# Two cross-attentions with keys projected into the heads' 8 channels, and quotients taken out of PSUM in all four

## The chip, the cores and the metric

The kernel runs on one core of a Trainium2 chip. The metric is the time of one execution on the device, in microseconds (us); the time before is the median of three runs.

## The reference

A tensor `x` of 32 batches x 56 tokens x 128 channels passes four layers. Each layer adds a cross-attention of its normalised tokens to a context of 32 batches x 1500 tokens x 64 channels, and then a feed-forward part. All four cross-attentions have 16 heads; their head width is 64, 8, 8 and 32. The second (the third is the same with biases):

```python
def _L1_xattn_ref(x, z, Wq, Wkv, Wo):        # x: 32 x 56 x 128, z: 32 x 1500 x 64
    Q = (x @ Wq.T).reshape(B, xN, 16, 8)
    KV = (z @ Wkv.T).reshape(B, zN, 2, 16, 8)
    K, V = KV[:, :, 0], KV[:, :, 1]
    attn = jax.nn.softmax(jnp.einsum('bqhd,bkhd->bhqk', Q, K) * 8 ** -0.5, axis=-1)
    return jnp.einsum('bhqk,bkhd->bqhd', attn, V).reshape(B, xN, 128) @ Wo.T

x = x + _L0_xattn_ref(_layernorm(x), ctx_512, ...)   # heads of 64
x = x + _L0_ffn_ref(_layernorm(x), ...)              # experts
x = x + _L1_xattn_ref(_layernorm(x), ctx_512, ...)   # heads of 8
x = x + _L1_ffn_ref(_layernorm(x), ...)              # int8 product
x = x + _L2_xattn_ref(_layernorm(x), ctx_512, ...)   # heads of 8, biases
x = x + _L2_ffn_ref(_layernorm(x), ...)              # Fourier
x = x + _L3_xattn_ref(_layernorm(x), ctx_512, ...)   # heads of 32
x = x + _L3_ffn_ref(_layernorm(x), ...)              # routed blocks
```

## The kernel before

The five engines' programs are written out by hand, with semaphores between them. Every float32 operand of a large product is held as a bf16 pair, high and remainder.

**Folded weights.** Before each cross-attention `pe_fold` multiplies every head's query weights with its key weights (line 242) and its value weights with its output weights (line 255). So a query has 64 channels per head, those of the context, and keys and values are the context itself. For heads of 8 channels too, a score is a sum over 64 context channels, and both parts of each pair count.

**A cross-attention** (`pe_cross`, `act_cross`, `dve_cross`, `pool_cross`, one queue of transfers in `sp_cross`) goes through 32 batches, each with 12 steps of 125 keys: 384 steps `T`, and two batches share a cycle of 24 steps, a pair. Columns are 16 heads x 56 queries = 896. In step `T`:

- TensorE takes up to two products (`product`) of a batch that comes later, then two halves of 448 score columns (`hf`), each by two matmuls: 128 rows (`cs`, high and remainder of the context, with the high queries `Qh`) and 65 rows (`chx` with the query remainders `Ql` and a row for the shift). Then it adds the values of step `T - 2`: for each of seven blocks of 128 columns, the high exponentials times 129 value columns (64 high, ones, 64 remainder), and the exponentials' remainder times 65.
- ScalarE takes the exponentials of both halves (line 751) into `pf`, one of three buffers.
- VectorE (line 823) and GpSimd (line 545) make the remainder `pl` of the exponentials of step `T - 1`; `JP` says how many of the seven blocks VectorE takes (5, 4, 4, 4). Both wait for both halves.

The products bound the scores from above, for the shift inside the exponential: a batch's 21 products of 500 columns (`PLAN`: for each of seven blocks a difference `d`, a sum `s` and a rest `r`) go through two PSUM banks. ScalarE turns the `d` (line 699), VectorE reduces `s` and `r` (lines 775, 778). The result is transposed, rounded and sent as one row into the query tile (line 436).

**The quotients of a batch.** The seven blocks of sums lie side by side in PSUM (129 columns each, over two banks, one set). After the last step of the batch ScalarE copies them out in two parts (lines 730, 731), GpSimd adds the halves (line 552), multiplies by the reciprocal that VectorE took (lines 802, 558), copies to bf16 (565) and makes the remainder (570). The first values of the next batch wait for the copies (`fc`). For the last batch VectorE does the four operations itself (lines 807 to 815). Transposes and the output product follow in a pair's later steps (`slot`), through PSUM bank 7, as do the projections of the queries: eight groups of two heads, three matmuls of 56 columns each, a fourth for the bias in the third cross-attention.

**Queries** go from `qch` and `qcl` to their place by six transfers a batch (`sp_spread`, lines 389 to 393), all on SP's queue, with the loads of `cs`, `chx` and the values `cnb` (lines 486 to 496). SP waits in the order of its program.

**Around it.** `pe_f1`, `act_f1` and `dve_f1` (the int8 part) also make the bias row `qbrow` of the third cross-attention (lines 1469, 1492). At the start SP loads inputs and the first weights and then the output bias (line 886), which the first `pe_fold` waits for.

Of the kernel before, what the change touches and what calls it, by code (L numbers as in the profile page):

```python
# [20 lines left out]
JP = (5, 4, 4, 4)  # L21
# [4 lines left out]
RND = 12582912.0  # L26

# [14 lines left out]
def build(nc, a, out):  # L42
    with ExitStack() as ctx:
# [54 lines left out]
        raw = [wst[:, 4032 + 903 * i:4935 + 903 * i].rearrange("p (j c) -> p j c", j=NJ) for i in range(2)]  # L98
# [8 lines left out]

        ctxN, ctxT = a["ctxN"], a["ctxT"]
# [7 lines left out]
        oneb = sb("oneb", [128, 64], BF16)  # L116
        qch, qcl = ([v[:, 12 + i, 0:448] for i in range(2)] for v in (Qh, Ql))
        qbrow = big[:, 6272:6784].bitcast(BF16)
# [112 lines left out]
        jobs1 = (0, 2, 4, 6, 10)  # L231
# [5 lines left out]
        def pe_fold(t, w, f, n, nd, wq, wk, wv, wo, weights, value):  # L237
            per = 512 // n
            w.wait_ge(weights, value)
            for j in range(H // per):  # L240
                for i in range(per):
                    r = t.matmul(bank(4 + j)[:, n * i:n * i + n], wq[0:nd, per * j + i, :], wk[0:nd, per * j + i, :],  # L242
                                 start=True, stop=True, skip_group_check=True)
                r.then_inc(s["f1"], 1)
            for j in range(4):
                k = fold_bank(f, n, j)
                if f in EARLY and j >= 2:
                    w.wait_ge(s["f1a"], FOLD_A[f])
# [10 lines left out]
        CLEAR_A1, CLEAR_MLP, CLEAR_F4 = 4, 11, 15  # L259
        EARLY = (1, 2)  # L260
        FOLD_A = (2, 6, 10, 12, 14)
# [39 lines left out]
        def act_fold(e, w, f, n):  # L301
            per, copies = 512 // n, 128 // n
            for j in range(1 if f == 3 else 0, H // per, 2 if f == 3 else 1):
# [23 lines left out]

        def pool_weights_low(g, w, f):
# [6 lines left out]
        def pool_fold(g, w, f):  # L335
            pool_weights_low(g, w, f)
# [45 lines left out]

        def sp_spread(y, w, ci, k):
            u, o = k % 2, k % QB
            w.wait_ge(s["pa"], B * ci + k + 1)
# [5 lines left out]
            w.wait_ge(s["pd"], B * ci + k + 1)  # L391
# [3 lines left out]
        def wait_spread_high(w, ci, k):  # L395
            w.wait_ge(s[f"qd_{k % 2}"], 64 * (B // 2 * ci + k // 2 + 1))

        def wait_spread_low(w, ci, k):
            w.wait_ge(s[f"ql_{k % 2}"], 32 * (B // 2 * ci + k // 2 + 1))
# [105 lines left out]
        def wait_tops(w, ci, k):  # L505
            w.wait_ge(s[f"lx_{k % 2}"], 16 * (ci * B // 2 + k // 2 + 1))
# [7 lines left out]
        def zeroed(ci):  # L514
            return 6 + 3 * ci if ci >= 0 else 0

        def pool_cross(g, w, ci):
            for k in range(2):
                g.memset(chx[k][64:65, :], 1.0).then_inc(s["zo"], 1)
                w.wait_ge(s["zo"], zeroed(ci - 1) + k + 1)  # L520
            for k in range(0 if ci else 3):
# [4 lines left out]
            for T in range(-36, NT + 11):  # L526
# [15 lines left out]
                if 0 <= T - 1 < NT:  # L542
                    r, at = (T - 1) % 3, 128 * JP[ci]
# [4 lines left out]
                if 0 <= (k := due(T, KT + 4)) < B - 1:  # L548
                    u, kb = k % 2, B * ci + k
                    r = raw[u][:, :, 0:C]  # L550
                    w.wait_ge(s["fc"], 2 * (kb + 1))
                    g.tensor_tensor(r, r, raw[u][:, :, C + 1:], ALU.add).then_inc(s["fp"], 1)  # L552
                    w.wait_ge(s["fp"], 4 * kb + 1)
                if 0 <= (k := due(T, KT + 7)) < B - 1:
                    u, kb = k % 2, B * ci + k
                    r = raw[u][:, :, 0:C]
                    w.wait_ge(s["rd"], kb + 1)
                    g.tensor_tensor(r, r, per_row(rden[u][:, :], C), ALU.mult).then_inc(s["fp"], 1)  # L558
                    w.wait_ge(s["fp"], 4 * kb + 2)
                if 0 <= (k := due(T, KT + 8)) < B - 1:  # L560
                    u, kb = k % 2, B * ci + k
                    r = raw[u][:, :, 0:C]
                    if k >= HB:
                        w.wait_ge(s["otr"], kb - HB + 1)
                    g.tensor_copy(O[:, k % HB, :, 0:C], r).then_inc(s["fp"], 1)
                    w.wait_ge(s["fp"], 4 * kb + 3)
                if 0 <= (k := due(T, KT + 10)) < B - 1:
                    u, kb = k % 2, B * ci + k
                    r = raw[u][:, :, 0:C]
                    g.tensor_tensor(O[:, k % HB, :, C:], r, O[:, k % HB, :, 0:C], ALU.subtract).then_inc(s["fp"], 1)  # L570
                    w.wait_ge(s["fp"], 4 * kb + 4)

        def pe_cross(t, w, ci, xh_, xl_, biased=False):
            t0, b0 = NT * ci, B * ci
            evac = (2 * NT + B) * ci

            def project(k):
                at = 128 * (k // 2) + 64 * (k % 2)
                hi, lo = xh_[:, at:at + NQ], xl_[:, at:at + NQ]
                for g in range(H // 2):  # L580
                    o = bank(7)[:, NQ * g:NQ * g + NQ]
                    if biased:
                        mm(t, o, qbrow[:, 128 * g:128 * g + 128], oneb[:, 0:NQ], True, False)
                    mm(t, o, wah2[:, g, :], hi, not biased, False)
# [21 lines left out]
            for T in range(-26, LAST):  # L606
# [26 lines left out]
                if 0 <= T - 2 < NT:  # L633
                    k, i = divmod(T - 2, KT)
                    r = (T - 2) % 3
                    ph = pf[r][0:KP, :].bitcast(BF16)[:, 1::2]
                    w.wait_ge(s["pl"], t0 + T - 1)
                    wait_values(w, ci, k)
                    if k:
                        w.wait_ge(s["fc"], 2 * (b0 + k) - 1)  # L640
                    for j in range(NJ):
                        if k and j == 3:
                            w.wait_ge(s["fc"], 2 * (b0 + k))
                        if j == JP[ci]:
                            w.wait_ge(s["plp"], NT * ci + T - 1)
                        cols = slice(128 * j, 128 * j + 128)
                        at = 2620 + 129 * j
# [1686 lines left out]
```

## Time and profile before

| | |
|---|---|
| median of three runs | 4035.7 us (4034.22 to 4037.05) |
| profiled execution | 4029.8 us, span from first to last instruction 4028.0 us |
| busy share of the span | TensorE 94%, VectorE 78%, ScalarE 66%, GpSimd 63% |
| mean granted TensorE clock | 0.954 |

The profile is one execution. A matmul's own time there includes its way through the array, so consecutive ones overlap in the record: what one costs is read from start to start. Busy times are unions of records; on VectorE and ScalarE too the end of one record may overlap the next one's start by some tens of ns. PEld are weight loads, beside matmuls. "Idle before" is the time that an engine stood still before a group, and what ended it.

### The profile page before, as it was taken

Reading aid. Unit: us, or ns where it says so; the run is one execution under the profiler, and the core shown is the slowest. Engines: PE = TensorE matmul, PEld = TensorE weight load, DVE = VectorE, ACT = ScalarE, POOL = GpSimd, SP = SyncE. Lnnn points to the kernel's source line nnn. Section 1 sums busy time; section 2 is a strip of 40 time slices with the busy share of each in tenths; the row PEclk is TensorE's granted clock in tenths of the full one; section 3 lists DMA queues with packets and bytes.
Section 4 is the critical chain, followed back from the end, with each engine's and each line's share of the span. In section 5 each row is a group of like instructions: output and inputs, shape, how many; then the busy total and the mean of one; then the engine's idle time right before and its main releaser. Section 6 shows DMA issues by size and latency. Waiting matters only on the chain.

```text
span 4028.0 us, 110585 instructions
## 1 busy us (share of the span) xinstructions
PE 3794.2 (94%) x43467; PEld 2887.3 (72%) x43467; DVE 3136.7 (78%) x6499; ACT 2673.5 (66%) x5365; POOL 2545.3 (63%) x2457
## 2 busy tenths in 40 slices
PE   6999999989979999999799999996997899999987
PEld 4777777766647777777577777775665677777765
DVE  6999999858888888887688887886654788888864
ACT  4887887756647777777377777772542577777752
POOL 4888888759856766677466766664001476676761
PEclk8999999979989999999699999997998899999998
DMA  5333333125432221221122122110000212222100
GB/s 130 104 110 111 112 107 109 41 90 159 142 111 57 60 61 54 60 61 43 28 60 61 54 61 61 54 56 19 3 1 18 65 54 64 57 58 63 55 22 15
DMA packets 157328, 266.80 MB, mean 66 GB/s; under 512 B 26632, under 2 KB 97432, under 8 KB 155432
## 3 DMA queue, kind: packets, MB, share of 16 engines
q1 hardware_dynamic: 156360, 259.67, 22.6%
q8 instruction: 343, 5.62, 0.6%
q14 instruction: 177, 1.45, 0.1%
q10 hardware_dynamic: 448, 0.06, 0.0%
HBM read 165.10 MB, written 50.26 MB: 53 GB/s over the span
## 4 chain that ended last, share of the span: by engine, by line
PE 87%; DVE 6%; POOL 2%; ACT 2%; DMA 1%; issue 1%; SPq 1%; POOLq 0%; DVEq 0%; ACTq 0%
PE ps L186 83%; PE ps L665 1%; DVE xn L166 1%; POOL wst L545 1%; PE ps L242 1%; DVE wst L823 1%; PE ps L255 1%; PE ps L1639 1%; DMA big<-big 1%; PE ps L1161 0%; DVE st L151 0%; DVE wst L778 0%; DVE relu L775 0%; ACT wb L324 0%; PE ps L193 0%
## 5 line engine op out<-in xcount | busy, mean ns | idle before, releaser
L545 POOL TENSOR_TENSOR wst<-wst 125x384 bf16<-125x384 f32 (+1 forms) x1536 | 1432.2, 932 | 833.1 <-ACT wst L751 772.3
L751 ACT ACTIVATE wst<-ps 125x448 f32<-125x448 f32 x3072 | 1518.1, 553 | 568.3 <-PE ps L186 553.8
L186 PE MATMUL ps<-big,cx 128*125 128x448 bf16 (+1 forms) x6144 | 1427.4, 353 | 0.7 <-DMA big<-topT 0.7
L186 PEld LDWEIGHTS ps<-cx,wst 125*128 125x128 bf16 x23040 | 1113.6, 98 | 307.5 <-POOL wst L545 15.2
L823 DVE TENSOR_TENSOR wst<-wst 125x512 bf16<-125x512 f32 (+1 forms) x1536 | 1270.2, 827 | 56.7 <-ACT wst L751 56.5
L186 PE MATMUL ps<-cx,wst 125*128 125x65 bf16 (+2 forms) x23040 | 1202.4, 204 | 12.1 <-POOL wst L545 11.6
L186 PEld LDWEIGHTS ps<-big,cx 128*125 128x125 bf16 (+1 forms) x6144 | 834.5, 137 | 283.9 <-issue 1.8
L186 PE MATMUL ps<-cx,big 128*128 128x500 bf16 (+1 forms) x2688 | 709.8, 317 | 10.2 <-DVE big L1744 2.6
L778 DVE TENSOR_REDUCE wst<-ps 128x1 f32<-128x500 f32 x896 | 604.5, 675 | 136.3 <-PE ps L186 123.6
L775 DVE CUSTOM_DVE_ANT_0 wst<-ps,wst 128x500 bf16<-128x500 f32 x448 | 302.9, 676 | 195.0 <-PE ps L186 150.5
L775 DVE CUSTOM_DVE_ANT_0 relu<-ps,relu 128x500 bf16<-128x500 f32 x448 | 302.1, 674 | 149.7 <-PE ps L186 81.4
L186 PE MATMUL ps<-diff,big 128*128 128x500 bf16 x896 | 342.7, 382 | 25.4 <-DMA big<-big 15.7
L699 ACT ACTIVATE wst<-ps 128x500 bf16<-128x500 f32 x448 | 270.9, 605 | 55.1 <-PE ps L186 55.1
L699 ACT ACTIVATE relu<-ps 128x500 bf16<-128x500 f32 x448 | 269.2, 601 | 45.3 <-PE ps L186 44.4
L182 POOL TENSOR_TENSOR rs<-ve,mhalf 128x8 f32<-128x8 f32 x26 | 43.6, 1677 | 395.5 <-DVE ve L161 379.7
L186 PEld LDWEIGHTS ps<-cx,big 128*128 128x128 bf16 x2688 | 202.2, 97 | 79.7 <-DVE wst L778 19.5
L570 POOL TENSOR_TENSOR big<-wst,big 128x448 bf16<-128x448 f32 x124 | 173.9, 1402 | 9.7
L186 PE MATMUL ps<-big 128*128 128x448 bf16 (+2 forms) x832 | 162.2, 353 | 4.2 <-POOL big L1056 2.3
L740 ACT ACTIVATE xn<-ps 128x896 bf16<-128x896 bf16 x128 | 122.3, 956 | 49.0 <-PE ps L665 48.4
L552 POOL TENSOR_TENSOR wst<-wst 128x448 f32<-128x448 f32 x124 | 146.0, 1177 | 9.7
L558 POOL TENSOR_TENSOR wst<-wst,rden 128x448 f32<-128x448 f32 x124 | 139.9, 1128 | 9.7
L186 PE MATMUL ps<-wb,xn 128*128 128x128 bf16 x2048 | 141.4, 225 | 4.0 <-ACT xn L740 4.0
(250 smaller groups left out, 4213.2 us busy)
## 6 DMA issues: line engine op xcount, KB each, us to landing
big<-big SPq DMA_DIRECT2D x768, 56.0 KB, 2.7
cx<-ctxT SPq DMA_DIRECT2D x96, 375.0 KB, 3.5
cx<-ctxN SPq DMA_DIRECT2D x64, 377.9 KB
cx<-in_ctxN SPq DMA_DIRECT2D x64, 375.0 KB
cx<-ctxT SPq DMA_DIRECT2D x96, 187.5 KB, 3.8
ctxN<-cx SPq DMA_DIRECT2D x32, 377.9 KB
ynN<-cx SPq DMA_DIRECT2D x32, 377.9 KB
cx<-ynN SPq DMA_DIRECT2D x32, 377.9 KB
```

Source lines behind the costliest of these rows:

```text
L182: g.tensor_tensor(rs[:, cols], ve[:, cols], mhalf[:, cols], ALU.pow).then_inc(s["pw"], 1)
L186: return t.matmul(o, l, r, start=start, stop=stop, skip_group_check=True)
L545: g.tensor_tensor(pl[r][0:KP, at:], pf[r][0:KP, at:], pf[r][0:KP, at:].bitcast(BF16)[:, 1::2], ALU.subtract).then_inc(s["plp"], 1)
L552: g.tensor_tensor(r, r, raw[u][:, :, C + 1:], ALU.add).then_inc(s["fp"], 1)
L558: g.tensor_tensor(r, r, per_row(rden[u][:, :], C), ALU.mult).then_inc(s["fp"], 1)
L570: g.tensor_tensor(O[:, k % HB, :, C:], r, O[:, k % HB, :, 0:C], ALU.subtract).then_inc(s["fp"], 1)
L699: e.activation(relus[n % 2], bank(max_bank(kb, k, item), 500), ACT.Relu).then_inc(s["half"], 1)
L740: e.activation(ob[p % 2][:, :, 64 * r:64 * r + NQ], bank(7).bitcast(BF16)[:, 0:HQ].rearrange("c (h q) -> c h q", h=H), ACT.Copy).then_inc( ...
L751: e.activation(pf[T % 3][0:KP, cols], bank(2 + n2 % 3, 448)[0:KP], ACT.Exp, scale=scale).then_inc(s["ev"], 1)
L775: v.tensor_tensor_reduce(out=half, in0=of, in1=half, scale=1.0, scalar=-3.0e38, op0=ALU.add, op1=ALU.max, accum_out=to[:, j, 0:1]).then_in ...
L778: v.tensor_reduce(to[:, j, 1:2], of, AX.X, ALU.max).then_inc(s["red"], 1)
L823: v.tensor_tensor(pl[r][0:KP, 0:to], pf[r][0:KP, 0:to], pf[r][0:KP, 0:to].bitcast(BF16)[:, 1::2], ALU.subtract).then_inc(s["pl"], 1)
```

## The change

1. In the second and third cross-attention (`ci` 1 and 2) the folding of queries with keys is left out. Keys are projected with `wks` into the heads' 8 channels: for each batch three parts of 500 keys, two matmuls each (`pe_keys`), a bf16 copy on ScalarE (`act_keys`) and a remainder on VectorE (`dve_keys`). Queries of a pair are projected by three matmuls of 128 columns.
2. Both go through HBM to change their layout: keys by two stores (`kD`) and three loads into 32 partitions each (`Ks`: high, remainder, high), queries by four stores of 112-byte pieces on a diagonal (`qD`, zeroed once at the start by eight stores) and the loads `Qm` and `Qs`. `Qm` is block-diagonal over the heads, for the products, whose other operand is the projected keys `KH`. A score is now one matmul of 97 rows for each group of four heads: four of 224 columns a step. The rows hold high x high, remainder x high, high x remainder and the shift.
3. In all four, high and remainder of the values are added into the same 65 columns: three matmuls of 65, 64 and 65 columns for each block. The seven blocks fit into one bank, and there are two sets, `acc`, for even and odd batches. VectorE takes the reciprocal and the quotients straight from PSUM, ScalarE copies them to bf16, GpSimd makes the remainder.
4. `SPLIT` gives VectorE 640, 448, 448 and 512 of the 896 remainder columns. In the two cross-attentions VectorE waits for the first half of the exponentials only, GpSimd for both.
5. The bias of the queries goes into the copies of the projected queries; the row `qbrow` and its work go.

```diff
-JP = (5, 4, 4, 4)
+SPLIT = (640, 448, 448, 512)
+        acc = [bank(5 + i, 65 * NJ) for i in range(2)]
...
             w.wait_ge(weights, value)
-            for j in range(H // per):
+            for j in range(0 if f in EARLY else H // per):
...
+        def pe_values(t, w, ci, T):
+            k, i = divmod(T, KT)
+            r, kb = T % 3, B * ci + k
+            ph, o, of = pf[r][0:KP, :].bitcast(BF16)[:, 1::2], acc[k % 2], cnb[k % 3]
+            w.wait_ge(s["pl"], NT * ci + T + 1)
+            wait_values(w, ci, k)
+            if kb >= 2:
+                w.wait_ge(s["fc"], kb - 1)
+            for j in range(NJ):
+                if 128 * j == SPLIT[ci] or j == 3 and SPLIT[ci] == 448:
+                    w.wait_ge(s["plp"], NT * ci + T + 1)
+                cols, at = slice(128 * j, 128 * j + 128), 65 * j
+                mm(t, o[:, at:at + 65], ph[:, cols], of[:, i, 0:65], i == 0 and j == 0, False)
+                mm(t, o[:, at:at + 64], ph[:, cols], of[:, i, 65:129], False, False)
+                n = mm(t, o[:, at:at + 65], pl[r][0:KP, cols], of[:, i, 0:65], False, i == KT - 1)
+            n.then_inc(s["pv"], 1)
+
+        def dve_values(v, w, ci, k):
+            u, kb = k % 2, B * ci + k
+            o = acc[u].rearrange("p (j c) -> p j c", j=NJ)
+            w.wait_ge(s["pv"], KT * (kb + 1))
+            v.reciprocal(rden[u][:, :], o[:, :, C]).then_inc(s["rd"], 1)
+            if k >= 2:
+                w.wait_ge(s["fp"], 2 * (kb - 1))
+            w.wait_ge(s["rd"], kb + 1)
+            v.tensor_tensor(raw[u], o[:, :, 0:C], per_row(rden[u][:, :], C), ALU.mult).then_inc(s["fc"], 1)
...
+        def act_values(e, w, ci, k):
...
+            e.activation(O[:, k % HB, :, 0:C], raw[k % 2], ACT.Copy).then_inc(s["fp"], 1)
...
+        KEY_SLOT = {21: (4, 0), 1: (2, 1), 4: (2, 2), 8: (3, 0), 12: (3, 1), 16: (3, 2)}
+        def head_slot(T):
+            p, i = divmod(T, 24)
+            for later, name in ((0, "keys"), (1, "keys split")):
+                if i - later in KEY_SLOT:
+                    more, c = KEY_SLOT[i - later]
+                    return (name, 2 * p + more, c) if 1 <= 2 * p + more < B else ("", 0, 0)
+            if i == 23 and 1 <= p + 2 < NP:
+                return "query", p + 2, 0
+            if i == 0 and 1 <= p + 1 < NP:
+                return "query split", p + 1, 0
+            if 1 <= p <= NP and i in (6, 7, 14, 15):
+                return ("turn", "turned")[i % 2], p - 1, 2 * p - 2 + (i >= 14)
+            if 1 <= p <= NP and i in (18, 19, 20):
+                return ("out 0", "out 1", "add")[i - 18], p - 1, 0
...
+        def sp_head(y, w, ci):
+            for T in range(-44, NT):
...
+                if (k := due(T, -18)) >= 0:
+                    w.wait_ge(s["pa"], projected(ci, "keys", k, 2))
...
+                    y.dma_start(kD[u, 0], KH[u]).then_inc(s[f"stT_{u}"], 16)
+                    w.wait_ge(s["pd"], projected_low(ci, "keys", k, 2))
+                    y.dma_start(kD[u, 1], KL[u]).then_inc(s[f"stT_{u}"], 16)
+                if (m := 0 if T == -44 else (T + 23) // 24 if (T + 23) % 24 == 0 and T > 0 else NP) < NP:
...
+                    w.wait_ge(s["pa"], projected(ci, "query", m))
+                    for v, of in enumerate((qhb, qlb)):
+                        for r in range(2):
+                            y.dma_start(diagonal(qD[2 * (m % 2) + r, v]), of[m % 2][:, 64 * r:64 * r + NQ]).then_inc(s[f"qd_{m % 2}"], 16)
+                        w.wait_ge(s["pd"], projected_low(ci, "query", m))
+                if (k := 0 if T == -44 else due(T, -22) or -1) >= 0:
+                    wait_query_stored(w, ci, k // 2)
...
+                    y.dma_start(Qm[k % 2], rows_of(qD[k % 4, 0])).then_inc(s[f"ql_{k % 2}"], 16)
...
+                if (k := due(T, -11)) >= 0:
...
+                    for n, v in enumerate((0, 1, 0)):
+                        y.dma_start(Ks[u][32 * n:32 * n + 32, :, 0:M], by_group(kD[u, v])).then_inc(s[f"lx_{u}"], 16)
...
+        def pe_keys(t, w, ci, k, c):
+            wait_keys(w, ci, k)
+            o, of = bank(keys_bank(k, c), 500), cs[k % 3][:, 500 * c:500 * c + 500]
+            mm(t, o, wkh, of, True, False)
+            mm(t, o, wkl, of, False, True).then_inc(s["pm"], 1)
...
+                    for hf in range(2):
+                        w.wait_ge(s["ev"], evac + n2 - 2)
+                        for g in (2 * hf, 2 * hf + 1):
+                            at = 4 * NQ * g
+                            r = mm(t, bank(2 + n2 % 3)[:, at - 448 * hf:at - 448 * hf + 4 * NQ],
+                                   Ks[u][0:97, g, KP * i:KP * i + 128], Qs[k % 3][0:97, at:at + 4 * NQ], True, True)
+                        r.then_inc(s["sc"], 1)
...
+                    w.wait_ge(s["ev"], evacuated(ci, T - 1) + 1)
+                    to = SPLIT[ci]
+                    v.tensor_tensor(pl[r][0:KP, 0:to], pf[r][0:KP, 0:to], pf[r][0:KP, 0:to].bitcast(BF16)[:, 1::2],
+                                    ALU.subtract).then_inc(s["pl"], 1)
...
             load_fold(y, s["w"], "L0", 64, 64)
+            w.wait_ge(s["idb"], 4)
+            for k in range(4):
+                for v in range(2):
+                    y.dma_start(rows_of(qD[k, v]), rowb[:, 0:HQ // 2].bitcast(BF16)).then_inc(s[f"qd_{k % 2}"], 16)
             w.wait_ge(s["idb"], 3)
             y.dma_start(crow[0:1, :], a["L0bo"]).then_inc(s["w"], 16)
...
-            pe_cross(t, w, 1, xTh, xTl)
+            pe_head(t, w, 1)
```

## Rows read from the trace of the kernel before

**Rows 1.** The page's first part: busy us, share of the span, instructions.
```profile
PE 3794.2 (94%) x43467; PEld 2887.3 (72%) x43467; DVE 3136.7 (78%) x6499; ACT 2673.5 (66%) x5365; POOL 2545.3 (63%) x2457
```

**Rows 2.** Windows of one pair each, of the second, third, first and fourth.
```profile
core 0: us, PE busy (x) PEld busy (x) DVE busy (x) ACT busy (x) POOL busy (x), PEclk, DMA share, GB/s
1406.58:1452.63 46.05, 46.05 (x595) 35.95 (x594) 37.44 (x78) 34.65 (x72) 32.18 (x33) 1.00 0.20 59
2225.29:2271.76 46.47, 46.47 (x612) 36.36 (x610) 37.44 (x78) 34.65 (x72) 32.18 (x33) 1.00 0.20 58
455.38:501.65 46.27, 46.21 (x596) 35.85 (x594) 42.47 (x78) 37.20 (x76) 38.35 (x41) 1.00 0.39 109
3462.18:3508.22 46.04, 46.04 (x596) 35.94 (x594) 37.43 (x78) 34.64 (x72) 32.16 (x33) 1.00 0.21 59
```

**Rows 3.** Chain of waits, second cross-attention: start us, us, what.
```profile
1406.58 5.43 PE ps L186 x63
1412.39 39.84 PE ps L186 x517
1452.63 5.42 PE ps L186 x63
```

**Rows 4.** Timeline of TensorE, second one: start us, us, instructions [merged].
```profile
1415.23 0.78 PE L186 MATMUL ps<-cx,wst 125*128 125x129 bf16 x15
1415.85 1.06 PE L186 MATMUL ps<-wb,xn 128*128 128x128 bf16 x16
1416.74 0.37 PE L186 MATMUL ps<-cx,big 128*128 128x500 bf16 x1
1416.95 0.93 PE L186 MATMUL ps<-big,cx 128*125 128x448 bf16 x4
1417.71 0.79 PE L186 MATMUL ps<-cx,wst 125*128 125x129 bf16 x15
...
1433.33 0.78 PE L186 MATMUL ps<-xT,wa 128*128 128x56 bf16 x24
1433.95 0.37 PE L186 MATMUL ps<-cx,big 128*128 128x500 bf16 x1
```

**Rows 5.** Groups by line in the second one's pair: count, busy us, mean ns.
```profile
L823 DVE TENSOR_TENSOR wst<-wst 125x512 bf16<-125x512 f32 x25 | 19.3, 774 | 0.0
...
L766 DVE TENSOR_TENSOR big<-ps,big 128x448 bf16<-128x448 f32 x2 | 1.2, 613 | 0.0
```

**Rows 6.** The same groups in the first one's pair.
```profile
L823 DVE TENSOR_TENSOR wst<-wst 125x640 bf16<-125x640 f32 x24 | 23.3, 972 | 0.0
```

**Rows 7.** Transfers in the second one's pair: count, size, median us to landing.
```profile
cx<-ctxT SPq DMA_DIRECT2D x2, 375.0 KB, 4.0
big<-big SPq DMA_DIRECT2D x12, 56.0 KB, 2.7
cx<-ctxT SPq DMA_DIRECT2D x2, 187.5 KB, 3.9
```

**Rows 8.** Chain of waits around the feed-forward parts and lead-ins.
```profile
815.58 7.05 PE ps L242 x32
...
1935.53 0.55 ACT wst L731
...
1950.60 7.05 PE ps L242 x32
...
1979.84 1.07 ACT big L1492 x2
1980.93 1.28 DVE big L1469 x2
...
2003.59 8.73 DMA big<-big
...
3149.38 9.79 DMA big<-big
```

**Rows 9.** The start: SP's timeline, and the chain of waits there.
```profile
7.83 0.43 SPq L886 DMA_DIRECT2D crow<-in_L0bo  x1
...
21.38 4.04 PE ps L242 x32
```

More of the change, by code:

```diff
@@ L26 @@
 RND = 12582912.0
+ONES = 1.0 + 127 / 65536
 class Gate:
@@ L302, in act_fold @@
             per, copies = 512 // n, 128 // n
-            for j in range(1 if f == 3 else 0, H // per, 2 if f == 3 else 1):
+            if f in EARLY:
+                w.wait_ge(s["w"], (0, 224, 336)[f])
+                e.activation(wqh, wqs[:, 0:128], ACT.Copy).then_inc(s["f1a"], 1)
+                e.activation(wkh, wks, ACT.Copy).then_inc(s["f1a"], 1)
+            for j in () if f in EARLY else range(1 if f == 3 else 0, H // per, 2 if f == 3 else 1):
                 if f == 4:
@@ new lines, in build, with projected, projected_low @@
+        HEAD_LAST = 24 * NP + 21
+        PROJECTED = [("keys", 0, 0), ("keys", 0, 1), ("keys", 0, 2), ("query", 0, 0)] + [
+            head_slot(T) for T in range(-26, HEAD_LAST) if head_slot(T)[0] in ("keys", "query")]
+        def projected(ci, what, p, c=0):
+            return projections(ci) + PROJECTED.index((what, p, c)) + 1
+        def projected_low(ci, what, p, c=0):
+            n = projected(ci, what, p, c)
+            return n if p else projections(ci) + (1 if what == "query" else c + 2)
@@ L850, in early_weights @@
         def early_weights():
-            return tuple(heads(15104 + 1024 * i, 8, n, big) for i, n in ((0, 128), (2, 64), (3, 64), (4, 128)))
+            return tuple(heads(15104 + 1024 * i, 8, n, big) for i, n in ((3, 64), (4, 128)))
         def load_fold(y, sm, n, d, width):
-            wq, wk, wv, wo = early_weights() if d == 8 else pre_weights(d, width)
+            if d == 8:
+                wv, wo = early_weights()
+                for name, v in (("q", wqs if n == "L2" else wqs[:, 0:128]), ("k", wks), ("v", wv), ("o", wo)):
+                    y.dma_start(v, a[n + name]).then_inc(sm, 16)
+                return
+            wq, wk, wv, wo = pre_weights(d, width)
             for name, v in (("q", wq), ("k", wk), ("v", wv), ("o", wo)):
@@ L1365, in pe_l1 @@
             wait_f0(w)
+            for c in range(3):
+                pe_keys(t, w, 1, 0, c)
             pe_turn(t, w, xn, s["xn"], 32, 1)
@@ L1513, in act_l2 @@
             wait_f1(w)
+            for c in range(3):
+                act_keys(e, w, 2, 0, c)
             act_turned_high(e, w, 4)
```

481 lines of the change are left out of this document (351 added, 130 removed).

## The prediction

> **What bounds the kernel now.** I read the page first: TensorE is busy for 94% of the span and VectorE for 78% [rows 1]. Then the windows of one pair of batches in each of the four cross-attentions: TensorE is busy for all of 46.05, 46.47 and 46.04 us in the second, third and fourth and for 46.21 of 46.27 us in the first, always at a granted clock of 1.00, which is the 2.4 GHz level [rows 2]. A cross-attention is 16 such pairs; the chain of waits repeats one pattern every 46.05 us, all of it matmuls [rows 3]. So these stretches are set by the number of columns that TensorE streams. In them VectorE is busy 37.4 us a pair, ScalarE 34.7, GpSimd 32.2 (first one: 42.5, 37.2, 38.4) [rows 2]. Whatever is taken from TensorE shows in full until VectorE, the next one, is full.
>
> **Prices on TensorE.** From start to start in its timeline [rows 4]: a 500-column product 0.21 us; the four 448-column score matmuls of a step 0.76 (0.190 each); the fifteen value matmuls of a step 0.62; sixteen 128-column ones 0.89 (0.0556 each); twenty-four 56-column ones, each with its own weights, 0.62 (0.026 each). These nearly lie on a line: (0.190 - 0.0556)/320 = 0.42 ns a column, with under 3 ns for the matmul itself.
>
> **TensorE in the second and third cross-attention, per pair (24 steps).**
> - Scores: four of 448 columns become four of 224. 224 columns lie on that line at 0.0556 + 96 x 0.00042 = 0.096 us; a step costs 0.38, not 0.76. 24 x 0.38 = 9.1 us saved.
> - Query projection: 48 matmuls of 56 columns (1.24 us) become three of 128 (0.17): 1.1 saved. The third also loses the bias matmuls, which is why its pair takes 0.42 us more today [rows 2].
> - Key projection is new: 2 batches x 3 parts x 2 matmuls of 500 columns = 12 x 0.213 = 2.6 us added.
> - Values: as many columns, 21 instructions a step for 15. By the 56-column row (0.46 ns a column all in) 1358 columns cost 0.63 us against 0.62. Bounds: nothing, or 6 x 0.026 = 0.16 us a step if each added pair of weight load and matmul costs a whole one. I take 0.012 a step, 0.3 a pair, since the row nearest in width is the lower one.
> - Sum: 46.05 - 9.1 - 1.1 + 2.6 + 0.3 = 38.7 us; the third comes to the same.
>
> A rule speaks against this split. The Trainium skill, "TensorE: Matmul & The Clock Gate", section "Back-to-back issue gap", gives 81 ns a matmul for a sustained stream of weight load and 128-column matmul. The trace disagrees: 0.89/16 = 56 ns, weights loaded each time [rows 4]. By the page's figure six more pairs would cost 6 x (81 - 56) = 0.15 us a step, about my upper bound.
>
> **VectorE there.** Today 37.4 us busy [rows 2]. Added: six remainders of 500 keys; the query remainder, the same operation on 448, takes 613 ns [rows 5], and 52 elements more at the 1.55 ns of the next item's slope make 0.69 at most: +4.0. Two quotients on 448 out of PSUM, by the same row 0.61 each: +1.2. Gone: two query remainders, -1.2; one 128-wide one comes, +0.3. The remainder of the exponentials shrinks from 512 to 448. 640 elements take 972 ns [rows 6], 512 take 774 [rows 5], so 64 fewer are 0.10 us less at that slope, or 0.067 at one element per cycle (the slope holds waits on GpSimd too): 24 x 0.085 = -2.0. Sum: 39.7 us, more than TensorE. ScalarE gets six key copies and loses two of its four PSUM copies and both query copies: about +2, so 37 us. GpSimd trades three operations a batch of about 1.1 us for 64 more columns in 24 steps: at most equal.
>
> So a pair can't take less than 38.7 us, and VectorE becomes the co-bound. What the two need together: products have two PSUM banks, so TensorE runs about one step ahead. The added work comes in lumps. VectorE's quotient and a key part fall on one step (2.5 us against 1.4 on TensorE); the output steps put 0.89 us on TensorE alone, twice in a row. Adding up both engines' work step by step over 24 steps, by these prices, their difference swings by about 1.9 us; a step of slack (some 0.8 us beyond latencies) leaves about 1.1 us of waiting. 39.7 + 1.1 = 40.8 us. Bounds: 38.6, if VectorE's busy time counts overlapping tails, and 43.5, if it needs all the idle time that it has today in the first cross-attention, 46.27 - 42.47 = 3.8 us [rows 2]; there TensorE doesn't wait, so all of it isn't needed.
>
> Gain: 16 x (46.05 - 40.8) + 16 x (46.47 - 40.8) = 84 + 91 = 175 us (bounds 88 and 245).
>
> **The queue of SP.** The queries now go to HBM (four stores a pair) and come back as the loads Qm and Qs; the keys go out in two stores of 384 KB and return as three loads into 32 partitions each, 14 transfers a batch for 10. Late first would be Qm of an even batch. Its queries are split at step 0, its product is due at step 7, about 11.4 us later. Between lie: the first store about 1 us after the split begins; four issues of 0.6; three issues of the other batch's keys, 1.8, ahead of it on SP; the wait that the stores have landed (2.7 us for 56 KB [rows 7], mostly beside those issues), then Qm's own issue and 4.0 us for a 375 KB load [rows 7]. That is about 1 + 2.4 + 1.8 + 0.8 + 0.6 + 4.0 = 10.6 us, plus what the 1.15 MB of keys hold it up. Waiting behind Qm on SP are the values, the next keys and the shift, all with slack of four steps or more; on TensorE everything waits for the product. I take it as just hidden, and 0 to 3 us a pair as the bounds. The Trainium skill, "SBUF — State Buffer", section "Door 1: The DMA port swizzle", says that a load into 32 partitions gets about half the bandwidth (189 GB/s): by that 6.1 us for these keys. Nearest here: half the bytes into 64 partitions land in 3.9 us against 4.0 [rows 7].
>
> **Elsewhere.**
> - Folds: the 16 query-key matmuls before the two feed-forward parts stand in the chain for 7.05 us each time [rows 8]. Gone: -14. The bias row's copies and remainders, 1.07 + 1.28 us, and half its matmuls also stand in the chain [rows 8]: -4.
> - End of each cross-attention: one ScalarE evacuation (0.55 us [rows 8]; the other overlaps) and two small operations less in a row: -1.3 x 4 = -5.
> - First and fourth: values +0.3 x 32 = +10 (bounds 0 to 120); the 0.2 us a pair by which the first exceeds the fourth at a batch's first values [rows 2] goes with two accumulators: -3. GpSimd's lighter load there I cost at nothing, since TensorE hides it; without that cover it could only gain.
> - Lead-in of the two: one more trip through HBM (+3), a shorter projection (-1.5) and queries ahead of the loads that make a spread land after 8.73 us today [rows 8], -4 in the third only: about -2 in all, bounds 6 either way.
> - Start: eight stores of zeros (8 x 0.6 us on SP) stand before the bias row, issued at 7.83 us today, that the first fold at 21.38 needs [rows 9]: +3, bounds 0 to 8.
>
> **Sum.** -175 - 18 - 5 + 10 - 3 - 2 + 3 = -190 us. The profiled execution took 4029.8 us (span 4028.0), 5.9 below the median of 4035.7. 4029.8 - 190 = 3840 us.
>
> **The rivals.**
> - Queries late every pair. For it: the round trip is as long as the time there is. If Qm lands after 8.7 to 9.8 us, as spreads behind 1.3 MB of loads do today [rows 8], it is 5 us late, of which the 1.1 us of waiting is swallowed: about 45 us a pair, 16 x (1.05 + 1.47) = 40 saved; with the other terms of the sum (-15) 3975 us. Against it: those rows are from a lead-in with four loads at once. 0.08.
> - Slower: both legs of that trip land so late (8.7 and 9.8 us). Then Qm is 11 us late and a pair takes 51.5 us: +168 instead of -175, 4183 us. It decides from 46.7 us a pair on, 6 to 7 us late. Against it: little else is queued when the stores are issued. 0.05.
> - Weight loads come into the open: 0.16 us a step in all four, 768 x 0.16 = +120 in the unchanged two, and 42.5 us a pair in the others: 16 x (3.55 + 3.97) = -120. With the rest (-18 - 5 - 3 - 2 + 3 = -25) 4005 us. The 56-column row stands against it. 0.03.
> - All hidden, TensorE alone bounds: 38.7 us a pair, 242 saved, 3773 us. 0.09. The forecast itself, 39.5 to 43.5 us: 0.75.
>
> **How the numbers follow.** Forecast 3840. 43.5 us a pair gives 3927, the upper bounds of start and lead-in some 10 more; a pair that waits 1 us for its queries on top of that 3955. Down: 38.7 with the other terms a little better, 3765. That leaves out slower, weights and most of late queries, under 0.2. About 0.2% (8 us) is what a measurement here can tell from no change. Slower 0.06: that rival, and 0.01 for weights and late queries together; same 0.02, out of the same two cases in part; faster 0.92.
>
> **What would show it.** Right: pairs of 40 to 42 us in the second and third, TensorE and VectorE both above 93% there, 24 x 4 score matmuls of 224 columns at 96 ns; 46.0 to 46.6 in the others; no 7.05 us fold at the two feed-forward starts. Wrong: TensorE waiting on the load of Qm at step 7; value groups above 0.65 us; VectorE's key remainders far above 0.69.

## The result, and the profile after

The changed kernel takes 3979.9 us (median of 4 runs, 3978.7 to 3983.5) against 4035.0 for the one before beside it: a ratio of 0.9863, 95% interval 0.9847 to 0.9879. It is faster, by 55 us where 190 were forecast: outside the range, on the slow side. Its profiled execution has a span of 3976.6 us, 51.4 less than before.

The page of the kernel after, part 1 (busy time, share of the span, instructions), answers to [rows 1]:

```profile
span 3976.6 us, 126748 instructions
PE 3630.8 (91%) x51275; PEld 2766.4 (70%) x51275; DVE 3270.3 (82%) x6773; ACT 2709.4 (68%) x5391; POOL 2100.8 (53%) x2087
```

The windows of one pair of batches after, in the second, third, first and fourth cross-attention, answer to [rows 2]:

```profile
core 0: us, PE busy (x) PEld busy (x) DVE busy (x) ACT busy (x) POOL busy (x), PEclk, DMA share, GB/s
1433.97:1478.29 44.32, 41.09 (x706) 32.24 (x706) 40.85 (x86) 36.36 (x76) 26.30 (x27) 1.00 0.54 143
2214.34:2258.72 44.38, 41.15 (x706) 32.24 (x706) 40.91 (x86) 36.39 (x76) 26.30 (x27) 1.00 0.54 143
472.31:519.29 46.98, 46.89 (x739) 36.59 (x738) 41.93 (x80) 36.75 (x74) 29.64 (x35) 1.00 0.38 107
3461.91:3508.63 46.72, 46.72 (x739) 36.63 (x738) 38.83 (x80) 34.26 (x70) 23.07 (x27) 1.00 0.20 58
```

Two things are to be seen. The pairs of the second and third came down by 1.7 and 2.1 us, not by 5.3 and 5.7, and neither TensorE (busy for 41.1 of 44.3 us) nor VectorE (40.9) is full there. The pairs of the first and fourth, where the change only touches values and quotients, went up by 0.7 us with TensorE still full.

Where the 51.4 us came from, cut at the first and last exponential of each cross-attention on ScalarE (where each starts, the loading of its table included; us):

| stretch | before | after | change | forecast, about |
|---|---|---|---|---|
| start | 64.4 | 68.4 | +4.0 | +3 |
| first cross-attention | 732.2 | 743.2 | +11.0 | +2 |
| up to the second | 405.7 | 410.7 | +5.0 | -7 |
| second | 729.1 | 699.8 | -29.3 | -84 |
| up to the third | 88.5 | 81.5 | -7.0 | -15 |
| third | 734.5 | 697.7 | -36.8 | -91 |
| up to the fourth | 412.2 | 407.7 | -4.5 | -1 |
| fourth | 728.3 | 736.4 | +8.1 | +5 |
| tail | 133.1 | 131.1 | -2.0 | -1 |

What ended TensorE's waits in the pair of the second (the waits of that window; in order: engine, line, what it waited for, total us, times, longest):

```profile
PEld ps L208 <- DVE wst L1155: 2.3, 3, 1.0
...
PEld ps L208 <- DVE wst L1158: 1.8, 3, 0.6
...
PEld ps L208 <- DVE wst L1185: 1.6, 3, 0.7
PE ps L208 <- DVE wst L1155: 1.5, 3, 0.8
DVE relu L1155 <- PE ps L208: 1.3, 2, 0.6
PE ps L208 <- DVE wst L1158: 1.2, 3, 0.5
DVE wst L1158 <- PE ps L208: 1.1, 3, 0.5
...
DVE wst L1155 <- PE ps L208: 0.6, 1, 0.6
```

TensorE (PE and its weight load, PEld, which wait together, so the two aren't added up) waits for VectorE's two reductions of products, L1155 and L1158, and less for its remainder, L1185. VectorE, in the same 44 us, waits for TensorE's products. No wait is for a transfer. Each engine is idle in part because the other was. The chain of waits of this pair, by line, says the same:

```profile
by line: PE ps L208 39.4%; DVE wst L1185 19.0%; DVE wst L1158 9.6%; issue 9.4%; DVE wst L1155 7.5%; DVE cTs L997 5.3%; DVE relu L1155 4.8%; DVE diff L1163 3.8%; DVE wst L626 0.7%; DVE rden L622 0.5%; DVEq L40 0.1%
```

Half of it lies on VectorE, whose program has remainders and key parts between the reductions. TensorE's timeline in this pair (start, us, form, count; the end of a row is modelled, so read from start to start):

```profile
1440.44 0.55 PE L208 MATMUL ps<-big 97*128 97x224 bf16 x4
1440.82 0.38 PE L208 MATMUL ps<-cTs,big 128*128 128x500 bf16 x1
1441.04 0.81 PE L208 MATMUL ps<-cx,wst 125*128 125x65 bf16 x21
1441.68 0.33 PE L208 MATMUL ps<-xT,wa 128*128 128x128 bf16 x3
1441.85 0.38 PE L208 MATMUL ps<-diff,big 128*128 128x500 bf16 x1
1442.06 0.55 PE L208 MATMUL ps<-big 97*128 97x224 bf16 x4
1442.97 0.38 PE L208 MATMUL ps<-cTs,big 128*128 128x500 bf16 x1 [0.35 <-DVE wst L1158]
```

Four scores of 224 columns take 0.38 us and the query projection 0.17, as priced. The 21 value matmuls take 0.64 where 0.63 was priced. With that, by an estimate from these starts, TensorE's own work is 38.7 + 24 x 0.016 = 39.1 us a pair, so it waits 5.2 of 44.3.

Ahead of the second cross-attention a stall is new. TensorE there, in the same columns:

```profile
1186.18 2.66 PE L208 MATMUL ps<-cx,wa 128*128 128x500 bf16 x6 [18.84 <-DMA cx<-ctxT]
1188.63 2.45 PE L215 MATMUL ps<-idf,xn 128*128 128x128 f32 x16
```

and the chain of waits (start, us, what):

```profile
1173.75 12.29 DMA cx<-ctxT
1186.18 2.66 PE ps L208 x6
1188.83 0.87 PE ps L215 x4
```

The projection of the first batch's keys stands in TensorE's order ahead of the transposes of the normalised input (L215), and waits for keys that land 12.29 us after their issue. VectorE had written the input by 1175.0 (sixteen operations from 1170.81, 4.19 us). Everything of the next stage waits 13.6 us (1175.0 to 1188.63) behind a transfer and a projection that only the keys need.

### The profile page after: what moved, and what is told of

It reads as the page before. It is cut to its first block, busy times and chain, and to the rows that moved or that the text cites. A ratio compares the mean times of both kernels' runs of the same rounds, so it can differ in the third digit from the quotient of the medians.

```text
span 3976.6 us, 126748 instructions
## 1 busy us (share of the span) xinstructions
PE 3630.8 (91%) x51275; PEld 2766.4 (70%) x51275; DVE 3270.3 (82%) x6773; ACT 2709.4 (68%) x5391; POOL 2100.8 (53%) x2087
## 4 chain that ended last, share of the span: by engine, by line
PE 65%; DVE 24%; issue 5%; DMA 2%; ACT 2%; POOL 2%; SPq 1%; DVEq 0%; POOLq 0%; ACTq 0%
PE ps L208 62%; DVE wst L1185 7%; DVE wst L1158 3%; DVE wst L1155 3%; DVE cTs L997 2%; DVE relu L1155 2%; DVE diff L1163 1%; DVE xn L188 1%; POOL wst L592 1%; PE ps L2004 1%; PE ps L710 1%; PE ps L275 1%; DMA big<-headq 1%; PE ps L1533 0%; PE ps L264 0%
## 5 line engine op out<-in xcount | busy, mean ns | idle before, releaser
L592 POOL TENSOR_TENSOR wst<-wst 125x448 bf16<-125x448 f32 (+2 forms) x1536 | 1410.1, 918 | 1252.9 <-ACT wst L790 642.3
L208 PE MATMUL ps<-cx,wst 125*128 125x65 bf16 (+1 forms) x32256 | 1246.2, 193 | 18.0 <-DVE wst L1185 12.3
L208 PE MATMUL ps<-big,cx 128*125 128x448 bf16 (+1 forms) x3072 | 714.4, 354 | 0.8 <-DMA big<-topT 0.8
L846 DVE TENSOR_TENSOR wst<-wst 125x640 bf16<-125x640 f32 (+1 forms) x768 | 646.8, 842 | 22.0 <-ACT wst L790 21.8
L1185 DVE TENSOR_TENSOR wst<-wst 125x448 bf16<-125x448 f32 x768 | 592.1, 773 | 4.3 <-ACT wst L1129 4.3
L208 PE MATMUL ps<-big 97*128 97x224 bf16 (+2 forms) x3872 | 582.7, 279 | 5.4 <-POOL big L1428 2.1
L208 PEld LDWEIGHTS ps<-big,cx 128*125 128x125 bf16 (+1 forms) x3072 | 417.3, 137 | 142.8 <-DMA big<-topT 1.6
L208 PEld LDWEIGHTS ps<-big 97*128 97x128 bf16 (+2 forms) x3872 | 374.9, 98 | 186.5 <-issue 4.4
L208 PE MATMUL ps<-cTs,big 128*128 128x500 bf16 x896 | 341.7, 384 | 39.4 <-DVE wst L1158 37.4
L208 PE MATMUL ps<-cx,big 128*128 128x500 bf16 (+1 forms) x1792 | 369.9, 286 | 7.3 <-DVE big L2109 2.6
L1158 DVE TENSOR_REDUCE wst<-ps 128x1 f32<-128x500 f32 x448 | 300.1, 670 | 33.2 <-PE ps L208 32.8
L1155 DVE CUSTOM_DVE_ANT_0 relu<-ps,relu 128x500 bf16<-128x500 f32 x224 | 150.5, 672 | 48.2 <-PE ps L208 41.2
L1155 DVE CUSTOM_DVE_ANT_0 wst<-ps,wst 128x500 bf16<-128x500 f32 x224 | 150.3, 671 | 37.6 <-PE ps L208 20.5
```

The costliest lines, as they stand in the source:

```text
L208: return t.matmul(o, l, r, start=start, stop=stop, skip_group_check=True)
L592: g.tensor_tensor(pl[r][0:KP, at:], pf[r][0:KP, at:], pf[r][0:KP, at:].bitcast(BF16)[:, 1::2], ALU.subtract).then_inc(s["plp"], 1)
L846: v.tensor_tensor(pl[r][0:KP, 0:to], pf[r][0:KP, 0:to], pf[r][0:KP, 0:to].bitcast(BF16)[:, 1::2], ALU.subtract).then_inc(s["pl"], 1)
L1155: v.tensor_tensor_reduce(out=half, in0=of, in1=half, scale=1.0, scalar=-3.0e38, op0=ALU.add, op1=ALU.max, accum_out=to[:, j, 0:1]).then_in ...
L1158: v.tensor_reduce(to[:, j, 1:2], of, AX.X, ALU.max).then_inc(s["red"], 1)
L1185: v.tensor_tensor(pl[r][0:KP, 0:to], pf[r][0:KP, 0:to], pf[r][0:KP, 0:to].bitcast(BF16)[:, 1::2], ALU.subtract).then_inc(s["pl"], 1)
```

## The experiments

The theories on the second and third cross-attention: **hand-over** (products have two PSUM banks; TensorE waits until VectorE has read one, VectorE until the next product stands, so TensorE's own 39.1 us and these waits add up); **VectorE's load** (with GpSimd's accesses beside it, VectorE is the bound); **queries late** (rival of the prediction, whose 3975 us happens to lie near the time that came out).

**Values and the order ahead of the heads** (one profiled run, 3964.5 us).

```
 ci 0: ph x of[0:65], pl x of[0:65], ph x of[65:129]      (low matmul last)
 ci 3: ph x of[64:129] in place of of[65:129]             (65 columns)
-    pe_keys x3, pe_turn, bias row, project(0)            (ci 1, 2; also on ScalarE)
+    pe_turn, bias row, project(0), pe_keys x3
```

> Three changes, each read in its own stretch. First cross-attention: the low value matmul (64 columns) goes behind the remainders' one, so that a group runs 65, remainder 65, 64. Fourth: the low matmul takes 65 columns, one too many, so its first output column is wrong there. Theory 'each added matmul has a constant of its own, some 4 ns': the pair stays at 46.98 us in the first and at 46.7 to 46.8 in the fourth. Rival 'a matmul of 64 columns just ahead of a change of weights is what costs': the 33 ns go down to 29 in both, and the pairs to about 46.3 and 46.1. Rival 'the weights in the remainders' tile come late': in the first the 33 ns stand ahead of the remainders' matmul again. Second and third cross-attention: the transposes of the normalised input and the first query projection come before the first batch's keys on TensorE and ScalarE. Theory 'the transposes wait behind keys that land after 12.3 us': from the last exponential of the first cross-attention to the first one of the second 10 to 18 us less than 410.7; the stretch between the second and the third, 81.5, changes by under 3, since its keys had landed long before. Rival 'the keys are on the path anyway': under 3 us less in both.

The pair stayed at 46.98 in the first and went to 46.81 in the fourth: neither the place nor the width of the low matmul is the cost. Up to the second cross-attention 398.6 us in place of 410.7, up to the third 79.8 in place of 81.5. On TensorE:

```profile
1169.30 4.23 PE L215 MATMUL ps<-idf,xn 128*128 128x128 f32 x16 [4.04 <-DVE xn L188]
...
1181.58 2.68 PE L208 MATMUL ps<-cx,wa 128*128 128x500 bf16 x6 [5.00 <-DMA cx<-ctxT]
```

The transposes no longer wait for the keys. What stayed on the path is the keys' own trip, so 12.0 of the 13.6 came back.

**Load taken off GpSimd and VectorE** (one profiled run, 3958.5 us).

```
 ci 1: g.tensor_tensor(pl[r][0:KP, at:at + 32], ...)      (was at:896)
 ci 2: dve_keys on 250 of 500 columns, from batch 2 on
```

> Left out: in the second cross-attention GpSimd computes 32 of its 448 columns of the exponentials' remainder (the rest of the tile stays as it was), in the third VectorE computes half of each key remainder (250 of 500 columns), from the third batch on. Theory 'VectorE's load sets the pace': every microsecond taken off VectorE shows in full. Second: its remainder falls from 770 to about 540 ns and the difference of keys from 868 to about 410, 24 x 0.23 + 2 x 0.46 = 6.4 us, so the pair falls from 44.3 until TensorE bounds, 39.2 to 40 us. Third: 6 x 0.26 = 1.6 us less, 42.8. Theory 'hand-over': TensorE and VectorE wait for each other in turn, as products have two banks; about half of what is taken from one comes back: 41 to 42 in the second, 43.6 in the third. If neither is true and transfers set the pace, both stay at 44.3.

Windows of a pair of the second and of the third in this run:

```profile
1435.97:1479.48 43.51, 41.05 (x707) 32.39 (x706) 38.65 (x85) 36.25 (x76) 8.88 (x27) 1.00 0.55 146
2200.00:2244.25 44.25, 41.16 (x710) 32.18 (x708) 40.26 (x85) 36.28 (x76) 26.15 (x27) 1.00 0.54 144
```

In the second VectorE's remainder fell from 770 to 616 ns, its busy time by 2.2 us (6.4 were expected; the difference of two key parts took 1290 ns in this window, where 868 were to become 410), and the pair by 0.8 (1.1 over the mean of the pairs). In the third the key remainders fell from 670 to 411 ns, 1.6 us in all, but the difference of key parts rose from 868 to 1129, so that VectorE's busy time fell by 0.65 us only; the pair fell by 0.13. Neither theory had these times: VectorE's load expected 39.2 to 40 and 42.8, hand-over 41 to 42 and 43.6. VectorE's busy time alone isn't the bound, since at 38.65 us of it the pair still takes 43.5. But it isn't free either: about half of the 2.2 us came back, a fifth of the waiting, and the run doesn't separate VectorE's shorter remainder from GpSimd's. That transfers set the pace, the third reading, fits the third cross-attention here, but not the waits above, nor the next run.

**A third product bank; less on TensorE** (one profiled run, 3916.6 us).

```
 ci 1: products in bank n % 3 (was n % 2), scores in bank 3 + n2 % 2 (was 2 + n2 % 3)
 ci 2: second matmul of pe_keys (wkl) left out from batch 1 on
```

> Second cross-attention: products rotate over three PSUM banks and scores over two (two and three before). Third: the second matmul of each key projection (the low half of the weights) is left out from the second batch on, 6 x 0.213 = 1.28 us off TensorE a pair. Theory 'VectorE's load sets the pace': both stay within 0.3 us of 44.3. Theory 'hand-over': with one more product ahead TensorE no longer waits for the bank that VectorE is reading, 41 to 42.5 us in the second; in the third about half of the 1.28 comes back, 43.7.

```profile
1420.00:1461.69 41.69, 40.73 (x708) 32.13 (x707) 40.13 (x85) 35.94 (x76) 26.45 (x27) 1.00 0.58 153
2160.00:2203.12 43.12, 39.95 (x701) 31.57 (x700) 40.77 (x85) 36.13 (x76) 26.32 (x26) 1.00 0.57 147
```

With not one operation less on any engine the second came down from 44.5 to 42.0 us (mean of its pairs), as the hand-over theory had it. TensorE's waits in two pairs of it (L1178 and L1175 are the reductions in this run, L1205 the remainder):

```profile
PEld ps L208 <- DVE wst L1205: 3.2, 6, 0.9
...
PEld ps L208 <- DMA big<-headq: 1.5, 2, 1.1
...
PEld ps L208 <- DVE wst L1178: 0.6, 2, 0.3
```

The weight loads' waits for reductions, 4.1 us in one pair with two banks, are down to 0.6 us in two; those for the remainder stayed, 3.2 in two pairs, and one for the load of the queries (big<-headq) is new. In the third 1.26 of the 1.28 us came back in the regular pairs (1.1 over all of them), more than the half expected: what TensorE does is on the path almost in full, what VectorE does in part.

**Another split of the remainder** (one profiled run, 3983.9 us): `SPLIT = (640, 512, 384, 512)`, VectorE waiting for both halves of the exponentials at 512.

> VectorE's share of the exponentials' remainder: 512 columns in the second cross-attention (it then has to wait for both halves of the exponentials, as before the change), 384 in the third (448 now). Theory 'VectorE's load sets the pace': 64 columns are 0.067 us, 24 x 0.067 = 1.6 us: 45.9 in the second, 42.8 in the third, unless GpSimd's longer share, 512 columns, slows VectorE by as much. Theory 'hand-over': the later start (one exponential, 0.54 us a step) is on the chain: above 47 in the second; 43.6 in the third. If GpSimd's share then is late for TensorE's fourth group of values, the third gets slower than 44.4.

44.5 us in the second, 44.4 in the third: 64 columns more or less, and a start of the remainder that is one exponential later, change 0.1 us. Neither theory had that in its numbers: hand-over expected above 47 and 43.6, VectorE's load 45.9 and 42.8. VectorE's busy time moved little, by +0.5 and -0.3 us, and each remainder took 787 ns for 512 columns and 716 for 384. By the second, the start of the remainder has a slack of about one exponential.

**Both repairs** (median of four runs): the new order and the third bank in both.

> The two repairs together: transposes and first query before the first keys in the second and third cross-attention, and three product banks with two score banks in both. If the two earlier results add up: 12 + 1.7 us from the order, 37.5 us from the banks in the second and as much in the third (44.4 to about 42.0 us a pair), so 3980 - 89 = about 3891 us. Rival: in the third the remaining waits stand at other steps, and its pair stays above 43: about 3905.

3890.9 us (3889.8 to 3894.4), ratio to before 0.9643, interval 0.9628 to 0.9657. The two gains add up as expected; the third's pair is 42.0 as well.

**Queries two steps earlier on top** (median of four runs).

```
-            if i == 23 ...: "query", p + 2      if i == 0 ...: "query split", p + 1
+            if i in (21, 22) ...: ("query", "query split")[i - 21], p + 2
             (first key part at step 23, store two steps and Qm two steps earlier)
```

> As the kernel with both repairs, and the queries of each pair are projected two steps earlier (step 21 in place of 23), stored two steps earlier, and their load Qm is issued two steps earlier. Theory 'with three banks the round trip of the queries is just late': TensorE's waits for the load of the queries (2.7 us in two pairs of the run with three banks) vanish and a pair takes 41.3 to 41.7 us, some 10 to 20 us less in all than the kernel without this. Rival 'the wait only changes its name': the pairs stay within 0.2 us, since TensorE then waits for VectorE, busy 40.3 of 42.0.

3887.5 us (3885.7 to 3889.8), 0.9635, interval 0.9619 to 0.9651: the lowest median of the kernels that compute everything, its runs below or level with those of the one without it. Its pairs are regular, 41.86 us:

```profile
1450.00:1491.86 41.86, 40.81 (x708) 31.90 (x706) 40.45 (x85) 35.86 (x75) 26.45 (x27) 1.00 0.58 152
```

The waits on Qm (1.5 us of the weight loads, as shown, in two pairs of the run that first had three banks) are gone, but the pair gained 0.1 at most, and of the 10 to 20 us little came. The rival, that the wait only changes its name, came out: TensorE's waits for the remainder and for the exponentials grew instead, from 3.5 and 1.2 us in two pairs of the run before to 3.8 and 2.3 (L1205 the remainder, L1149 the exponentials, L1178 a reduction):

```profile
PEld ps L208 <- DVE wst L1205: 3.8, 6, 0.9
...
PEld ps L208 <- ACT wst L1149: 2.3, 10, 0.3
...
PEld ps L208 <- DVE wst L1178: 0.6, 2, 0.3
```

**The same loads with three banks** (one profiled run, 3883.2 us): the second run's cuts, and in the values of the fourth the low matmul reads the high columns, in the first the matmuls stand in three blocks.

> With both repairs; left out as in the second run: in the second cross-attention all but 32 of GpSimd's 448 columns of the remainder, in the third half of each of VectorE's key remainders. In the fourth the low value matmul multiplies the high columns 0 to 63 again (its output is wrong there); in the first the seven high, seven low and seven remainder matmuls stand in three blocks. 'With the third bank VectorE's load is the next bound': the third falls by most of 1.6 us a pair (40.6 from 42.0; with two banks it was 0.13), the second to TensorE's own 39.2 or to the queries' trip, 40 to 41. 'TensorE's own work and fixed latencies set it all along': the third stays within 0.3 us of 42.0. Values: if the columns that the low matmul reads are what costs 33 ns, it takes 29 in the fourth and the pair 46.1; if it is a constant of that matmul, 46.7 stays. In the first 46.98 stays if the order doesn't matter.

A window of the second:

```profile
1450.00:1491.70 41.70, 40.98 (x710) 32.45 (x709) 38.33 (x85) 36.31 (x77) 9.26 (x26) 1.00 0.58 152
```

Mean pairs 41.8 in the second and 41.9 in the third. In the second VectorE was busy for 38.3 us in place of 40.4, and the pair gained about 0.2. So at 42 us too VectorE's busy time by itself isn't the bound. The test isn't clean: this run has the queries at their old place, and the weight loads' waits for them in the second grew from 7.6 us in the run with both repairs to 12.9 (from the second pair on), so part of a gain may be hidden there. In the third VectorE's busy time fell by 0.6 us and the pair by less than 0.1. The low matmul on other columns: 46.55 for 46.72, between the two times expected; three blocks: 46.83 for 46.98.

**Controls** (one profiled run, 3963.7 us), with two product banks.

```
 ci 1, 2: queries two steps earlier     ci 1: scores in two banks
 ci 3: ph x of[0:129] (7 matmuls) + pl x of[0:65] (7), 14 in place of 21
```

> Controls, from the changed kernel with its two product banks. Both heads' cross-attentions: queries projected, stored and loaded two steps earlier. Second: scores rotate over two PSUM banks in place of three, the third stays empty. Fourth: each group of values is 14 matmuls, seven of 129 columns (placed over one another, so the output is wrong there) and seven of 65. Theory 'TensorE's own work plus the hand-over of product banks': third unchanged, 44.4 within 0.2 us, second 44.3 to 45 (fewer score banks can't help). Rival 'queries late every pair': the third falls towards 42. Rival 'two score banks alone made the gain': the second falls to 42. Values: if the number of matmuls costs the 0.7 us a pair, the fourth falls from 46.72 to about 46.0; if it is the second accumulator or the remainders' tile, it stays.

```profile
1420.00:1464.30 44.30, 41.77 (x711) 31.76 (x708) 41.13 (x85) 36.16 (x76) 26.01 (x27) 1.00 0.55 144
2160.00:2204.27 44.27, 41.15 (x707) 32.19 (x705) 41.15 (x85) 36.37 (x75) 26.38 (x27) 1.00 0.54 143
3461.00:3507.04 46.04, 46.04 (x571) 35.87 (x570) 38.70 (x80) 34.22 (x70) 23.12 (x27) 1.00 0.20 58
```

Earlier queries alone give 0.1 us (the third), so the queries were not late. Two score banks, without a third product bank, give nothing more (the second). Fourteen value matmuls in place of 21, with the same columns, bring the fourth back to 46.04, its time before: 0.68 us for 24 x 7 = 168 matmuls, 4.0 ns each.

**Less on TensorE with three banks** (one profiled run, 3872.6 us): from the kernel with the earlier queries, key remainders halved in the second, wkl left out in the third.

> From the kernel with both repairs and the earlier queries (41.86 us a pair in both). Left out: in the second cross-attention half of each of VectorE's key remainders (1.6 us a pair), in the third the second matmul of each key projection (1.28 us of TensorE). Theory 'TensorE's own work plus waits of fixed length': second 41.6 to 41.9, third 40.6 to 40.8. Theory 'with three banks the load of VectorE, busy for 40.4 of 41.9, bounds': second 40.3 to 40.8, third 41.6 to 41.9.

```profile
1450.00:1491.70 41.70, 40.47 (x705) 31.74 (x703) 40.04 (x85) 35.87 (x75) 26.30 (x27) 1.00 0.57 152
2150.00:2190.90 40.90, 39.89 (x703) 31.41 (x700) 39.83 (x85) 35.62 (x77) 26.32 (x27) 1.00 0.59 155
```

(These two windows are 0.2 and 0.1 us short of the pairs.) The second stayed at 41.9 from pair to pair; VectorE's busy time fell by 0.4 us there, not by 1.6. The third fell from 41.9 to 41.0: 0.9 of 1.28, where 40.6 to 40.8 was expected. TensorE's own work still decides most; its longest wait is now for the remainder (L1208 in this run), the next for the exponentials (1.2 us):

```profile
PEld ps L208 <- DVE wst L1208: 2.3, 6, 0.9
```

## Why the prediction was wrong

- **TensorE per pair, 38.7 us: right to 1%.** Scores and query projections cost what their rows said; with values as measured the sum is 39.1.
- **What the two engines need together, +1.1 us: this step failed.** I took VectorE's 39.7 us as the floor and added a small swing, with "a step of slack (some 0.8 us beyond latencies)". VectorE was busy for 40.85 us, near enough, but it stood idle for 3.5 us of the pair itself, and the pair didn't follow its busy time. The step of slack wasn't there: TensorE waits 5.2 us, in about two thirds of its recorded waits because a product's bank comes free only when VectorE has reduced it, and products have two banks. A third bank gave back 2.4 us without less work anywhere, and these waits all but vanished. With two banks 2.2 us off VectorE's busy time (and GpSimd's load with it) gave 1.1, with three 2.1 gave 0.2. The 2.8 us that TensorE still waits with three banks, for the remainder and the exponentials above all, weren't taken apart. Before the change TensorE was busy for all of the pair, so a product's trip was covered; I read it as uncovered by the halved scores, which give a product half the time until the next (argued from the rows; no run put the long scores back). 44.4 against 40.8 us a pair is 16 x 2 x 3.6 = 115 of the 135 us that were missing. The bound of 43.5 came from the first cross-attention's idle time on VectorE, a sum of busy time again, and so wasn't one.
- **VectorE's prices.** The 448-wide remainder took 770 ns, no less than the 774 of 512 columns before, where I took 0.085 off; the key remainder 670 as priced (0.69). The difference of key parts, 868 ns where the one before took 408, wasn't in the sum. What these cost in time no run shows by itself.
- **Values, +0.3 a pair: mis-sized,** 0.7 measured in the first and fourth, 22 us in place of 10. Each of the added matmuls costs 4.0 ns. It lay within the bounds (0 to 3.75 a pair), nearest to nothing, as taken; the rival by which weight loads come into the open (0.16 us a step) is refuted: 0.03 was measured. The Trainium skill's 81 ns a matmul ("TensorE: Matmul & The Clock Gate", section "Back-to-back issue gap") would, by the prediction's estimate, have made it 0.15 a step; the trace, with 0.03, differs.
- **The first one's stall, -3: didn't come.** Its pair still exceeds the fourth's by 0.26 us, as before by 0.23.
- **Folds, -14, and the bias row: half right.** The query-key matmuls of 7.05 us [rows 8] are gone from both chains. Ahead of the third, from the last exponential to the first split of the transposed input, 59.6 us became 49.2, so 10.4 us came of the 12 forecast for fold, bias row and the end of the cross-attention. Ahead of the second, the input was written 12.4 us earlier than before (363.4 us after the last exponential in place of 375.7), but its first split came at 378.7 in place of 375.7, since the keys' transfer and projection stood in between; taking them away gave 12.0. I had costed the lead-ins after the transposes and not looked at what was moved ahead of them in TensorE's order. That part, first split to first exponential, rose by 1.9 and 3.4 us, 5.3 in all where -2 was forecast, with 6 either way as bounds.
- **The queue of SP: right in its outcome, not in its sizes.** The page's DMA issues (KB each, median us from issue to landing) answer to [rows 7]:

```profile
big<-headk SPq DMA_DIRECT2D x192, 375.0 KB, 5.4
headk<-cTs SPq DMA_DIRECT2D x128, 375.0 KB, 3.7
cx<-ctxT SPq DMA_DIRECT2D x96, 375.0 KB, 10.0
...
big<-headq SPq DMA_DIRECT2D x64, 224.0 KB, 7.0
```

Qm took 7.0 us where I had put 4.0, and the loads of the context 10.0 where the page before had 3.5. All were hidden at 44.4 us, where TensorE waits for queries 0.2 and 0.3 us in the whole of the second and third after the first pair; Qm first showed in the run with three banks. The rival's number came near the result by chance; its mechanism is refuted by the waits and by the control.
- **Start +4.0, within 0 to 8;** from run to run of the changed versions it moved between 65.9 and 70.1. The stretch up to the fourth (407.3 to 412.1) and the tail (129.4 to 132.0) move as much, so the -1 us forecast for each can't be read from them.

Open: why the value group's low matmul gets 0.17 us a pair cheaper when it reads other columns, and what would take the rest of the waits. A fourth product bank could take little: with three, TensorE's weight loads wait 0.6 us in two pairs for reductions. A third score bank beside three product banks wasn't tried.

## What to carry to other kernels

When the engine that sets the pace gets less to do, the next bound need not be the second busiest engine; it can be a hand-over that the old work covered. Follow one buffer from its writer through all its readers back to the writer, with what stands ahead of each reader in its engine's order, and count the buffers. (No sum of this kind was worked out here; that the number of buffers mattered here was shown by adding one.) Busy shares can't show it: VectorE was busy for over 90% with two banks as with three, and the same operations took 2.4 us a pair less. And wherever work moves ahead of a stage in an engine's order, ask what it waits for: here the whole next stage waited 13.6 us behind it in TensorE's order.

## What the runs showed of the hardware

Small matmuls have a price of their own at the full granted clock (1.00): 168 more of them over the same columns cost 0.68 us, 4.0 ns each, with weights loaded for each; with the same number, other columns or another order made it 0.17 and 0.15 us less. VectorE's remainder between two SBUF operands (448 columns) took 770 ns beside GpSimd's like operation on the other 448 and 616 ns when that was cut to 32 columns.
